# Moving one chunk's normalisation, some stores and one signal, and cutting a GpSimd addition in four, in a long-convolution and feed-forward block

## What is computed

```python
xn = (x - mean) / sqrt(var + 1e-5)
proj = xn @ in_proj_w + in_proj_b            # 256 -> 768
v = proj[..., :256]
for i in range(2):                           # two long convolutions
    v = fft_conv(v, filter_i)                # filter from a small MLP with exp(-|decay| t) window
    xc = depthwise_conv3(ctrl_i) + kb        # ctrl_i is the i-th other third of proj
    v = v * (xc * sigmoid(xc @ gate_w[i] + gate_b[i]))
attn = v @ out_proj_w + out_proj_b
tern(w), scale(w) = clip(round(w / s), -1, 1), s = mean(|w|, axis=1)
h = xn @ (tern(w_fc) * scale).T + gate * (xn @ v.T @ fast_b.T @ u.T)
ffn = relu(h)**2 @ (tern(w_proj) * scale).T
out = x + attn + ffn
```

## Time and profile before

| | us |
|---|---|
| three runs | 881.22, 882.63, 882.59 |
| median | 882.59 |
| the profiled execution | 882.74 |
| its span in the trace | 880.8 |
| TensorE busy | 837.3 (95%) |
| VectorE busy | 621.8 (71%) |
| ScalarE busy | 471.4 (54%) |
| GpSimd busy | 238.6 (27%) |

### The profile page before, as it was taken

One profiled execution on the slowest core, in us unless ns is written; L12 is line 12 of the kernel. 1 busy time (PEld: TensorE's weight loads), 2 busy tenths in 40 slices (PEclk: granted clock), 3 DMA queues, 4 the chain that ended last, 5 costly groups with the idle time before them and its releaser, 6 DMA issues.

```text
span 880.8 us, 25943 instructions
## 1 busy us (share of the span) xinstructions
PE 837.3 (95%) x9920; PEld 695.4 (79%) x9921; DVE 621.8 (71%) x1041; ACT 471.4 (54%) x698; POOL 238.6 (27%) x248
## 2 busy tenths in 40 slices
PE   8779999999999997999999999999999999999997
PEld 3468888888888866878888888777887787788997
DVE  7849988988999884565665566566546656666887
ACT  6757777787877763444435353434444444444221
POOL 4445646655664402021112112111011201200000
PEclk9989999999999999999999999999999999999999
DMA  8762243234323268768767778677887876952896
GB/s 217 235 217 97 96 149 138 95 103 162 116 95 138 102 165 242 156 138 196 173 162 156 189 167 197 124 168 181 181 151 171 180 174 115 202 111 47 221 314 209
DMA packets 90687, 142.03 MB, mean 161 GB/s; under 512 B 12861, under 2 KB 70606, under 8 KB 89742
## 3 DMA queue, kind: packets, MB, share of 16 engines
q1 hardware_dynamic: 72990, 101.80, 48.7%
q0 software_dynamic: 7728, 28.05, 10.0%
q10 hardware_dynamic: 9920, 11.54, 4.0%
HBM read 97.39 MB, written 43.97 MB: 160 GB/s over the span
## 4 chain that ended last, share of the span: by engine, by line
PE 47%; DVE 9%; issue 4%; ACT 1%; DMA 1%; DVEq 0%; POOL 0%; ACTq 0%; POOLq 0%
PE pp L1372 13%; PE py L1391 13%; PE pf L1341 11%; DVE r L1163 3%; PE pf L1347 3%; PE py L1428 2%; PE py L1359 2%; DVE pp L1153 2%; DVE r_lo L1168 1%; DVE GC L1158 1%; DVE xb L1158 1%; PE pp L457 1%; PE pp L459 1%; PE pp L458 1%; ACT r_hi L1275 1%
## 5 line engine op out<-in xcount | busy, mean ns | idle before, releaser
L1275 ACT ACTIVATE r_hi<-r 128x512 fp32r<-128x512 f32 x128 | 80.9, 632 | 149.4 <-DVE r L1163 149.4
L1391 PEld LDWEIGHTS py<-vwin,lead 64*64 64x64 f32 x5120 | 132.9, 133 | 25.2 <-issue 25.2
L1372 PE MATMUL pp<-wproj,r_hi 128*128 128x256 f32 x512 | 135.3, 297 | 14.6 <-DVE r_lo L1168 10.4
L1270 ACT ACTIVATE r<-pf,fscale 128x512 f32<-128x512 f32 x128 | 87.8, 686 | 111.5 <-PE pf L1347 111.4
L1391 PE MATMUL py<-vwin,lead 64*64 64x128 f32 (+4 forms) x5120 | 146.9, 265 | 0.5 <-issue 0.5
L1168 DVE TENSOR_TENSOR r_lo<-r,r_hi 128x512 fp32r<-128x512 f32 x128 | 93.1, 727 | 67.2 <-ACT r_hi L1275 67.1
L1341 PE MATMUL pf<-tokens,split_a 128*128 (+1 forms) x512 | 139.6, 394 | 0.9 <-issue 0.9
L1372 PE MATMUL pp<-wproj,r_lo 128*128 128x256 f32 x512 | 126.7, 281 | 0.0
L1372 PEld LDWEIGHTS pp<-wproj,r_hi 128*128 128x128 f32 x512 | 96.1, 188 | 32.1 <-DVE r_lo L1168 14.3
L498 POOL TENSOR_SCALAR lead<-lead,norms 128x256 f32<-128x256 f32 x64 | 117.8, 1851 | 3.4 <-POOL norms L492 3.4
L660 DVE SCALAR_TENSOR_TENSOR xc<-ctrl,taps,xc 128x512 f32<-128x512 f32 x128 | 96.8, 776 | 18.8 <-ACT xc L766 18.1
(11 more groups left out here) (189 smaller groups left out, 1531.1 us busy)
## 6 DMA issues: line engine op xcount, KB each, us to landing
lead<-filters SPq DMA_DIRECT2D x128, 320.0 KB, 6.2
xnT_hbm<-split_b SPq DMA_DIRECT2D x32, 512.0 KB, 3.3
tokens<-xnT_hbm POOLq DMA_DIRECT2D x30, 512.0 KB, 5.1
lead<-in_attn_x SPq DMA_DIRECT2D x16, 512.0 KB, 4.1
gc_hbm<-xc SPq DMA_DIRECT2D x16, 512.0 KB, 2.6
GC<-gc_hbm SPq DMA_DIRECT2D x32, 256.0 KB, 6.3
out<-GC ACTq DMA_DIRECT2D x15, 512.0 KB, 6.4
GC<-in_attn_x POOLq DMA_DIRECT2D x9, 512.0 KB, 7.5
```

The source lines that it names most:

```text
L1270: act.activation(r[j][:, :], pf[:, j, :], ACT.Relu, scale=fscale[:, m:m + 1]).then_inc(relu_done, 1)
L1275: act.activation(r_hi[j][:, :], r[j][:, :], ACT.Copy).then_inc(r_hi_done, 1)
L1372: last = pe.matmul(pp[:, i, :], part[m % 2][:, i * P:(i + 1) * P], wproj[:, m, :], start=(m == 0 and n == 0 and i % 2 == 0), stop=(m == HT ...
L1391: last = pe.matmul(py[g % 2][q * BW:(q + 1) * BW, side, l, :, A:NB], tile[rows, q * PAIR + l, j * BW:(j + 1) * BW], vwin[g % 2][rows, q, l ...
```

## The change

In setup, the statistics of chunk 1 are taken by VectorE and its normalisation is done by GpSimd, which gets the second set of small values (`norms0`) for chunk 0; the step before the first of the project stage loses both. ScalarE takes the sums of |w_fc| for three of eight row tiles, VectorE for five, and GpSimd the thresholds. The low part of chunk 0 is made after the ternary values of w_proj, and ScalarE copies both halves of the turned w_proj. The scales and v_t are stored from parts of GC1 that no load of the next stage writes, in a new order, and are counted with the large stores (`STORES`), which the project stage waits for later; SyncE waits only for the two stores of zeros. In mix, `y_out` is raised ahead of the memsets, the wait for `srow_in` goes into `scale`, and GpSimd's bias addition becomes four instructions of 128x256.

```diff
-STORES = 10
+STORES = 12
...
-        srow = sb("scale_row", [1, D])
+        srow = Gf[0:1, 7 * L + 7 * HID // 4:7 * L + 7 * HID // 4 + D]
...
-        vrank = sb("vstack", [P, KT, PARTS, RANK], F32R)
+        vrank = Gf[:, 7 * L + 3 * HID // 2:7 * L + 3 * HID // 2 + KT * HALF].bitcast(F32R).rearrange("p (k s r) -> p k s r", k=KT, s=PARTS)
+        norms0 = sb("norms0", [P, TT, 11])
...
+        ACT_SUMS = 3
...
-            sp.wait_ge(srow_ready, 1)
-            load(scales, srow[0:1, :], small_stored)
-            sp.wait_ge(vrank_ready, 1)
-            load(v_t, vrank[:, :, :, :].bitcast(F32), small_stored)
             sp.wait_ge(ranks_ready, 1)
             load(u_t, ranks.bitcast(F32), stored)
             by_input_row = projT.rearrange("p (m d) -> p m d", m=HT)
...
+            sp.wait_ge(proj_ready, 1)
+            load(proj_t[:, 0:HT // 2, :], by_input_row[:, 0:HT // 2, :], stored)
+            sp.wait_ge(srow_ready, 1)
+            load(scales, srow, stored)
+            sp.wait_ge(vrank_ready, 1)
+            load(v_t, vrank.bitcast(F32), stored)
+            sp.wait_ge(proj_ready, 2)
+            load(proj_t[:, HT // 2:HT, :], by_input_row[:, HT // 2:HT, :], stored)
+            sp.wait_ge(small_stored, 16 * 2)
             sp.wait_ge(proj_in, 16 * PROJ_LOADS)
...
+            pool.wait_ge(abs_summed, ACT_SUMS)
+            pool.wait_ge(fc_summed, 1)
+            pool.tensor_scalar(fsc[:, :], fsc[:, :], 1.0 / D, 1e-5, ALU.mult, ALU.max).then_inc(uscale_step, 1)
+            pool.wait_ge(uscale_step, 1)
+            pool.tensor_scalar(fth[:, 0:HT], fsc[:, :], 0.5, None, ALU.mult).then_inc(uscale_step, 1)
+            pool.tensor_scalar(fth[:, HT:2 * HT], fsc[:, :], -0.5, None, ALU.mult).then_inc(uscale_step, 1)
+            rstd0(pool, 0, True)
+            normalise0(pool, 0, 0)
...
+            rstd(pool, 1)
+            normalise(pool, 1, 1)
...
-            statistics(dve, 0, 0, True)
             dve.wait_ge(fc_in, 16)
-            link(dve.tensor_reduce(fsc[:, :], fc_nat, AX.X, ALU.add, apply_absolute_value=True))
-            scales_of(fsc, fth, HT, D)
+            dve.tensor_reduce(fsc[:, ACT_SUMS:HT], fc_nat[:, ACT_SUMS:HT, :], AX.X, ALU.add, apply_absolute_value=True).then_inc(fc_summed, 1)
+            statistics0(dve, 0, 0, True)
+            statistics(dve, 1, 1, True)
+            dve.wait_ge(uscale_step, 3)
+            below(fc_nat, fc_tern, fth, HT, slice(0, D))
             dve.reciprocal(finv[:, :], fsc[:, :]).then_inc(finv_ready, 1)
-            below(fc_nat, fc_tern, fth, HT, slice(0, D))
             dve.wait_ge(filter_in, 16 * FILTER_LOADS)
-            link(dve.tensor_scalar(ndec[:, :], dec[:, :], -1.0, None, ALU.mult))
-            link(dve.tensor_tensor(ndec[:, :], ndec[:, :], dec[:, :], ALU.min))
+            link(dve.scalar_tensor_tensor(out=ndec[:, :], in0=dec[:, :], scalar=-1.0, in1=dec[:, :], op0=ALU.mult, op1=ALU.min))
...
-            dve.wait_ge(xn_hi_done, 1)
-            dve.wait_ge(xnT_done, 1)
-            dve.tensor_tensor(xn[1][:, :, :], xnT[:, :, :], xn[0][:, :, :].bitcast(F32), ALU.subtract).then_inc(xn_split, 1)
             for h in range(2):
                 cols = slice(h * HID // 2, (h + 1) * HID // 2)
                 below(pr_nat, pr_tern, pth, KT, cols)
                 above(pr_nat, pr_tern, pth, KT, cols)
+            dve.wait_ge(xn_hi_done, 1)
+            dve.wait_ge(xnT_done, 1)
+            dve.tensor_tensor(xn[1][:, :, :], xnT[:, :, :], xn[0][:, :, :].bitcast(F32), ALU.subtract).then_inc(xn_split, 1)
...
-            dve.wait_ge(projT_mm, 2)
-            dve.wait_ge(proj_ready, 1)
-            dve.tensor_copy(projT[:, L // 2:L], lower[:, L // 2:L]).then_inc(proj_ready, 1)
...
+            act.wait_ge(fc_in, 16)
+            for m in range(ACT_SUMS):
+                act.activation(h1[:, m * D:(m + 1) * D], fc_nat[:, m, :], ACT.Abs, accum_out=fsc[:, m:m + 1]).then_inc(abs_summed, 1)
...
-            act.wait_ge(projT_mm, 1)
-            act.activation(projT[:, 0:L // 2], lower[:, 0:L // 2], ACT.Copy).then_inc(proj_ready, 1)
+            for h in range(2):
+                cols = slice(h * L // 2, (h + 1) * L // 2)
+                act.wait_ge(projT_mm, h + 1)
+                act.activation(projT[:, cols], lower[:, cols], ACT.Copy).then_inc(proj_ready, 1)
...
             pe.wait_ge(xnT_done, 1)
-            pe.wait_ge(xn_split, 1)
+            pe.wait_ge(xn_hi_done, 1)
...
-                if s0 + 2 < NCH:
+                if 0 <= s0 and s0 + 2 < NCH:
                     rstd(pool, s + 2)
                     normalise(pool, s + 2, s0 + 2)
...
                 if s0 < 0:
-                    statistics(dve, 1, 1)
...
-                pool.tensor_tensor(buf, buf, bo_row[:, :].unsqueeze(1).broadcast_to([P, TT, D]), ALU.add).then_inc(xb_biased, 1)
+                for i in range(TT):
+                    row = buf[:, i, :]
+                    last = pool.tensor_tensor(row, row, bo_row[:, :], ALU.add)
+                last.then_inc(xb_biased, 1)
...
-            for rows in (ranks, zs):
-                dve.memset(rows[HALF:P, :].bitcast(F32), 0.0).then_inc(rest_zero, 1)
+            dve.sem_inc(y_out, 2)
             dve.memset(lowmask[:, :], 0.0).then_inc(mask_zero, 1)
             dve.wait_ge(mask_zero, 1)
             dve.memset(lowmask[2 * RANK:3 * RANK, :], 1.0).then_inc(mask_ready, 1)
-            dve.sem_inc(y_out, 2)
+            for rows in (ranks, zs):
+                dve.memset(rows[HALF:P, :].bitcast(F32), 0.0).then_inc(rest_zero, 1)
...
-            dve.wait_ge(srow_in, 16)
-
             def scale(it):
+                dve.wait_ge(srow_in, 16)
                 dve.wait_ge(proj_mm, it * HT + HT + 2)
```

More of the change, by code:

```diff
@@ L49, with setup_stage @@
 HALF = PARTS * RANK
-def setup_stage(nc, hbm, ident, bv_row, flag, V, GC1, Wv, Win, Wgate, eps, half, load_x, load_taps, norm, tern, ranks, fscale, stored, xn, xnT, x0, xn_ready, first_done):
+def setup_stage(nc, hbm, ident, bv_row, flag, V, GC1, Wv, Win, Wgate, eps, half, load_x, load_taps, norm, norms, tern, ranks, fscale, stored, xn, xnT, x0, xn_ready, first_done):
     (in_w, in_b, out_b, freqs, w1, b1, w2, b2, w3, b3, decay, gate_w, fast_b, w_fc, w_proj, u, v, gate,
@@ L130, in setup_stage @@
         projT_mm, proj_ready, srow_mm, srow_ready = sem("projT_mm"), sem("proj_ready"), sem("srow_mm"), sem("srow_ready")
-        psum_ready, psc_ready, finv_ready, uscale_step = sem("psum_ready"), sem("psc_ready"), sem("finv_ready"), sem("uscale_step")
+        abs_summed, psc_ready, finv_ready, uscale_step = sem("abs_summed"), sem("psc_ready"), sem("finv_ready"), sem("uscale_step")
+        fc_summed = sem("fc_summed")
+        ACT_SUMS = 3
         x0T = ps[:, 4:4 + KT, :]
@@ L134, in setup_stage @@
         hi_ready, eps_ready, vrank_ready = sem("hi_ready"), sem("eps_ready"), sem("vrank_ready")
-        statistics, rstd, normalise = norm
+        statistics0, rstd0, normalise0 = norm(norms0)
+        statistics, rstd, normalise = norm(norms)
         ctx.enter_context(nc.allow_non_contiguous_dma(reason="a few small vectors, one value a partition"))
@@ L360, in _ @@
             for k in range(KT):
-                act.activation(junk[:, k, :], pr_nat[:, k, :], ACT.Abs, accum_out=psc[:, k:k + 1]).then_inc(psum_ready, 1)
+                act.activation(junk[:, k, :], pr_nat[:, k, :], ACT.Abs, accum_out=psc[:, k:k + 1]).then_inc(abs_summed, 1)
             act.wait_ge(xT_mm, 1)
@@ L367, in _ @@
             act.wait_ge(m1_mm, 1)
-            act.activation(vrank[:, :, :, :], ps[:, 6, 0:KT * RANK].rearrange("p (k r) -> p k r", k=KT).unsqueeze(2).broadcast_to([P, KT, PARTS, RANK]),
+            act.activation(vrank, ps[:, 6, 0:KT * RANK].rearrange("p (k r) -> p k r", k=KT).unsqueeze(2).broadcast_to([P, KT, PARTS, RANK]),
                            ACT.Identity, scale=gcol[:, :]).then_inc(vrank_hi_done, 1)
@@ L1519, in conv_ffn_kernel @@
             dve_passed, pool_passed = (weights.enter_context(nc.semaphore(n)) for n in ("dve_norm_passed", "pool_norm_passed"))
-            norm = norm_steps(xt, norms, eps, half, x_loaded, stat_done, aggr_done, rstd_step, xn_ready, dve_passed, pool_passed)
+            norm = lambda values: norm_steps(xt, values, eps, half, x_loaded, stat_done, aggr_done, rstd_step, xn_ready, dve_passed, pool_passed)
             bias_in = weights.enter_context(nc.semaphore("bias_in"))
@@ L1563, in conv_ffn_kernel @@
             peaks = weights.enter_context(nc.sbuf_tensor("peaks", [P, 2, 4], F32))
-            setup_stage(nc, hbm, ident, bv_row, flag, V, GC1, Wv, Win, Wgate, eps, half, load_x, load_taps, norm,
+            setup_stage(nc, hbm, ident, bv_row, flag, V, GC1, Wv, Win, Wgate, eps, half, load_x, load_taps, norm, norms,
                         xm[:, 0, :, :, :].rearrange("p s k t -> p (s k t)"), xm[0:HALF, 1, 0, :, :].rearrange("p k t -> p (k t)"), fscale, stored, xn, xnT, xt[0], xn_ready, first_done)
```

(2 more changed lines are left out.)

10 lines of the change are left out of this document (4 added, 6 removed).

## The result

The changed kernel takes 871.76 us, median of 870.36 to 874.30 over four runs, against 882.61 before: ratio 0.9883, 95% interval 0.9854 to 0.9913. That is 10.9 us faster; 868 was forecast, 14.5 faster. The profiled execution took 873.15 us, with a span of 871.2 against 880.8. Runs of one kernel lie further apart than I had assumed: 3.9 us over these four, and 10.8 us (875.23 to 886.00) over 23 runs of the kernel before on another chip. So for anything under 2 us I look at traces, and at several of them where I can, since each trace is one execution.

A forecast was written before the change was run, and what follows sets the result against it. The prediction took TensorE's idle time as the bound: waits for VectorE's low part in mix and the borders into project and mix. Terms 8.6 + 1.9 + 4.0 = 14.5 us off 882.74 gave 868, range 863.5 to 874.

The forecast's parts named there:

- 42.9 + 0.84: Border from setup to project: setup ends at 42.9 instead of 46.94 us, and the border itself costs 0.84.
- A square is held until GpSimd's addition ends, and the pieces let VectorE in: Mix stage: a blocked square waits for the rest of one piece only; 7 to 10 us come back, 8.6 taken.
- the example: Mix iteration at 728.81 us: square 1.87 us late, 1.41 reaching TensorE; with pieces 0.22 late, about 0.3 reaching TensorE.
- Mix start, 1.9 us: Border into mix: early `y_out` saves 1.2 to 1.7 us, and L1172's wait of 0.45 goes too.
- Setup, 4.0 us: Setup's end: rearranged work and stores end the stage at 42.9 instead of 46.94 us; bounds 2.5 to 5.8.
- Sum: Whole kernel: 8.6 + 1.9 + 4.0 = 14.5 us against the profiled 882.74, so 868.
- the mix term: Mix stage: the gain from the bias addition in four pieces, 8.6 us.
- rival 2: Border to project: GpSimd or something placed too early ends setup, giving 0.5 to 2 us, 870.5 to 872; chance 0.14.
- Rivals 1 and 3: Mix: pieces hold VectorE as one, 877 to 882, chance 0.16; the same with dear pieces, slower, up to 899, 0.05.

The follow-up runs named there:

- the timed kernel without the pieces: The changed kernel with GpSimd's bias addition in one piece again: 880.72 us over 12 runs, ratio 0.9992 (0.9972 to 1.0012).
- the two-piece run: The changed kernel with the bias addition in two instructions of 128x512 instead of four of 128x256: 872.95 us, ratio 0.9891.
- the kernel with eight: The changed kernel with the bias addition in eight instructions of 128x128 instead of four of 128x256: 869.34 us, ratio 0.9864.

## Why the start of mix gave nothing

**The signal and the moved wait alone,** in the kernel before:

```diff
-            for rows in (ranks, zs):
-                dve.memset(rows[HALF:P, :].bitcast(F32), 0.0).then_inc(rest_zero, 1)
+            dve.sem_inc(y_out, 2)
             dve.memset(lowmask[:, :], 0.0).then_inc(mask_zero, 1)
             dve.wait_ge(mask_zero, 1)
             dve.memset(lowmask[2 * RANK:3 * RANK, :], 1.0).then_inc(mask_ready, 1)
-            dve.sem_inc(y_out, 2)
+            for rows in (ranks, zs):
+                dve.memset(rows[HALF:P, :].bitcast(F32), 0.0).then_inc(rest_zero, 1)
...
-            dve.wait_ge(srow_in, 16)
-
             def scale(it):
+                dve.wait_ge(srow_in, 16)
```

> The kernel before with y_out ahead of the memsets and the wait for the scales in scale, nothing else. Theory (TensorE cannot begin the mix stage earlier, whatever the signal does): its first product comes 3.40 us after its last one, as before, and the time is within 1 us of the kernel before. Rival (the signal does set it, and something else in the full change takes it back): the first product 1.5 us earlier and 1.5 to 2 us gained.

Measured: ratio 1.0003 (0.9983 to 1.0024). The timeline:

```profile
336.01 1.51 PE L1358 MATMUL py<-tokens,split_b 128*64 128x512 f32 x3 [3.41 <-issue]
```

3.41 us again, in twelve profiled executions between 3.40 and 3.52 where no spare product stood ahead. The rival falls.

**What holds TensorE there?** First probe: three spare products of 512 columns at the start of its mix block and three behind the branch (`pe.If(tail < 1)`), in the changed kernel.

```diff
...
+            for _ in range(3):
+                pe.matmul(pf[:, 0, :], ident[:, :], Vprobe, start=True, stop=True)
             pe.sem_inc(fc_mm, HT)
...
             tail = pe.value_load(flag[0:1, 0:1], min_val=0, max_val=1)
...
             def stages(far):
+                for _ in range(3):
+                    pe.matmul(pf[:, 1, :], ident[:, :], Vprobe, start=True, stop=True)
```

> The changed kernel with three spare products at the very start of TensorE's mix block and three more behind its branch on the flag, none waiting for a semaphore. Theory (TensorE has to read the flag and take a branch, and what follows it comes late): the first three start about 1.5 us after the last product of the project stage, the other three only with rank, 3.4 us or more after it. Rival (rank waits for data, the tokens or vrank): all six come early, and only rank starts 3.4 us after.

```profile
332.21 2.81 PE L1342 MATMUL pf<-GC,ident 128*128 128x512 f32 x6 [1.43 <-PEq L524]
334.86 2.74 PE L1464 MATMUL pf<-GC,ident 128*128 128x512 f32 x6
```

The first three do start 1.43 us after the stage before, but they last so long that the next three follow without a gap, and the probe hides what it was to show. It took 876.30 us in its one run. I made the second with eight columns a product and four places.

```diff
...
+            pe.matmul(pf[:, 0, 0:8], ident[:, :], spare, start=True, stop=True)
             pe.sem_inc(fc_mm, HT)
...
             def stages(far):
+                pe.matmul(pf[:, 0, 0:8], ident[:, :], spare, start=True, stop=True)
...
                 pe.wait_ge(vrank_in, 16)
+                if first:
+                    pe.matmul(pf[:, 0, 0:8], ident[:, :], spare, start=True, stop=True)
                 pe.wait_ge(y_out, it * GPI + 2)
                 if first:
+                    pe.matmul(pf[:, 0, 0:8], ident[:, :], spare, start=True, stop=True)
                     pe.wait_ge(first_in, 32)
```

> The changed kernel with four spare products of eight columns on TensorE: at the start of its mix block, behind the branch on the flag, behind rank's wait for vrank, and behind its wait for y_out. Theory (reading the flag and branching): the first starts 1.4 us after the last product of the project stage, and the second, third and fourth together 3.3 us after it, with rank right behind. Rival (data): the second comes before 2.5 us, and one of the later gaps holds the rest; which one names the wait.

```profile
330.80 0.36 PE L1341 MATMUL pf<-GC,ident 128*128 128x8 f32 x2 [1.43 <-PEq L524]
332.70 0.59 PE L1465 MATMUL pf<-GC,ident 128*128 128x8 f32 x2 [1.54 <-issue]
333.14 0.57 PE L1369 MATMUL pf<-GC,ident 128*128 128x8 f32 x2
333.56 0.57 PE L1372 MATMUL pf<-GC,ident 128*128 128x8 f32 x2
333.99 1.95 PE L1379 MATMUL py<-tokens,split_b 128*64 128x512 f32 x4
```

Behind the border's 1.43 us, the whole delay lies between the first and the second: 332.70 - 330.80 = 1.90 us. The waits for vrank, `y_out` and the tokens cost nothing; each later product follows at the pace of the probe. 1.43 + 1.90 = 3.33, which is the 3.40 but for 0.07. What TensorE's sequencer does in the 1.90 us stands in the same trace, under the lines of the source (ns, shortest, median, longest, then the start):

```profile
L1342 PEldq EVENT_SEMAPHORE  x1: 51/51/51, 330.8 to 330.8; - x1
L1345 PEldq TENSOR_LOAD <-flag x1: 890/890/890, 331.3 to 331.3; - x1
L1345 PEldq FUSED_REGOPS  x1: 168/168/168, 332.2 to 332.2; - x1
L1482 PEldq COMPARE_BRANCH  x2: 86/1972/3858, 332.6 to 862.6; - x2
```

About 0.5 us go to the first probe and three semaphore signals (from L1342 on), 0.89 us to the load of the flag, 0.4 to working on the register, and 0.09 to the branch, the first of the two at L1482. So it is the load above all. In the kernel before the same load took 0.858 us, in the changed kernel 0.867. The Trainium skill (Runtime: NRT & Kernel Launch, "Instruction fetch mechanics") says that a taken branch to a target outside the fetched window forces a fetch. No such fetch shows here: the branch starts at 332.6 and the next product at 332.70.

## Why setup gave so little

The profile shows SyncE late with its issues. Four runs take the possible causes apart.

**Normalisation back in the project stage,** in the changed kernel:

```diff
-            rstd(pool, 1)
-            normalise(pool, 1, 1)
...
-                if 0 <= s0 and s0 + 2 < NCH:
+                if s0 + 2 < NCH:
```

> The changed kernel with GpSimd's normalisation of chunk 1 back in the step ahead of the project stage. Theory (DMA backlog): SyncE's last issues are as slow as in the changed kernel, the first product stays between 46 and 47.5, time within 1 us. Rival (GpSimd's normalisation slows SyncE's issues, or its end sets the border): issues of 0.3 to 0.7 us and a first product before 44.5.

Measured: 871.03 us, ratio 0.9890 (0.9854 to 0.9925). SyncE's queue and the first product:

```profile
38.44 1.96 SPq L146 DMA_DIRECT2D u_t<-tokens  x1
40.44 2.10 SPq L146 DMA_DIRECT2D proj_t<-GC  x1
42.59 1.86 SPq L146 DMA_DIRECT2D scales<-GC  x1
```

```profile
47.15 0.76 PE L469 MATMUL pc<-split_b,split_a 128*128 128x512 f32 x1 [8.00 <-PEq L55]
```

As slow without GpSimd at work. Moving the normalisation neither helps nor harms, within the error.

**The last four stores from ScalarE's queue,** in the changed kernel:

```diff
-            sp.wait_ge(proj_ready, 1)
-            load(proj_t[:, 0:HT // 2, :], by_input_row[:, 0:HT // 2, :], stored)
...
             act.activation(sigmoid_table[:, :], eps[:, 0:1], ACT.Sigmoid)
+            act.wait_ge(proj_ready, 2)
+            for h in range(2):
+                ms = slice(h * HT // 2, (h + 1) * HT // 2)
+                act.dma_start(proj_t[:, ms, :], by_input_row[:, ms, :]).then_inc(stored, 16)
+            act.wait_ge(srow_ready, 1)
+            act.dma_start(scales, srow).then_inc(stored, 16)
+            act.wait_ge(vrank_ready, 1)
+            act.dma_start(v_t, vrank.bitcast(F32)).then_inc(stored, 16)
```

> The changed kernel with the last four stores of setup (both halves of proj_t, the scales, v_t) issued from ScalarE's queue after its last activation. Theory (SyncE's issues are slow because the DMA engines are behind with the filters' stores, whatever queue asks): the four issues take long from ScalarE's queue too, more than 1 us each for the large ones, and the first product of the project stage comes at 45 or later. Rival (only SyncE's own queue is full): they take 0.3 to 0.7 us each, and the first product comes near 44.5.

Measured: 871.73 us, ratio 0.9901 (0.9863 to 0.9938). ScalarE's queue:

```profile
39.73 2.18 ACTq L385 DMA_DIRECT2D proj_t<-GC  x2
41.96 1.92 ACTq L387 DMA_DIRECT2D scales<-GC  x1
43.92 0.85 ACTq L389 DMA_DIRECT2D v_t<-GC  x1
```

The store of 1 KB takes 1.92 us to issue from this queue too. It is not SyncE's queue alone that is full. Of the forecast, the first product at 45 or later came (45.52). The two large ones took over 1 us on average, but not each: 0.35 and 1.80 us one by one.

I read it as a backlog of the DMA engines. Their share is 0.99 from 38 to 42 before and 0.98 after, so they are as busy in both kernels. From 24 to 46 they moved 5.63 MB before and 5.99 MB after, nearly all of it the filters, fc_t, u_t and proj_t. The change asks for the transfers earlier and without a pause, and they do not come much faster. Not every small store is slow: with the same setup stage, the 1 KB took between 0.29 and 1.78 us to issue, and the border came at 45.74 and 46.05 in the two traces with 0.29. What stays is the sum of the issues. Which part of the engines' path holds an issue is open.

**The four stores deferred.** In the variant with the normalisation back, they are issued in the project stage, behind the first two stores of xn, where `stored` is waited for only later.

```diff
-            sp.wait_ge(proj_ready, 1)
-            load(proj_t[:, 0:HT // 2, :], by_input_row[:, 0:HT // 2, :], stored)
-            sp.wait_ge(srow_ready, 1)
-            load(scales, srow, stored)
-            sp.wait_ge(vrank_ready, 1)
-            load(v_t, vrank.bitcast(F32), stored)
-            sp.wait_ge(proj_ready, 2)
-            load(proj_t[:, HT // 2:HT, :], by_input_row[:, HT // 2:HT, :], stored)
+            later.append(lambda sp: [sp.dma_start(dst, src).then_inc(stored, 16) for dst, src in (
+                (proj_t[:, 0:HT // 2, :], by_input_row[:, 0:HT // 2, :]), (proj_t[:, HT // 2:HT, :], by_input_row[:, HT // 2:HT, :]),
+                (scales, srow), (v_t, vrank.bitcast(F32)))])
...
+                if s0 < 0:
+                    load_ahead[3][0](sp)
```

> The changed kernel with the normalisation of chunk 1 back in the project stage and the last four stores of setup issued there too, behind the first two stores of xn. Theory (the border waits for SyncE to get rid of these issues): the first product comes at 42 to 43, 4 to 5 us earlier, TensorE idles about 3.5 us instead of 8 and has at most as many slow products, and 3.5 to 5.5 us are gained over the changed kernel, 866 to 868. Rival (the stores come back in the project stage, as late loads or a late wait for `stored`): less than 1 us gained.

Measured: 867.22 us (864.81 to 871.46), ratio 0.9847 (0.9814 to 0.9881), on the chip where the variant without deferring took 871.03: 3.8 us less (the intervals of the two ratios overlap; five of the six runs lie below all four of the other variant). The queue and the first product:

```profile
44.87 2.49 SPq L199 DMA_DIRECT2D proj_t<-GC  x2
```

```profile
41.92 0.47 PE L464 MATMUL pc<-split_b,split_a 128*128 128x512 f32 x1 [3.17 <-PEq L55]
```

The issues are as slow as ever, and no border waits for them. The border stands at 41.92, 5.2 us earlier than in the changed kernel's trace and 3.8 us earlier than in any other with the changed setup, and 1.8 us ahead of the 42.9 + 0.84 of the prediction. So the issues are what held the border. This kernel has the lowest median of the study.

**Six spare products at the end of setup,** in that kernel, to keep the clock up:

```diff
+            pe.wait_ge(ranks_ready, 1)
+            for _ in range(6):
+                pe.matmul(ps[:, 4, :], ones[:, :], h2[:, 0:512], start=True, stop=True)
```

> The kernel with deferred stores (defer_norm_back) and six spare products of 512 columns on TensorE at the end of setup, whose results nobody reads. Theory (the idle time ahead of the project stage is what takes the clock down there): the granted clock stays at 1.00 over the border, the nine or so products at half the clock are gone, and 1.5 to 2 us more are gained, ratio about 0.983. Rival (the clock falls there anyway, or the products delay the border): the same number of slow products, no gain.

```profile
38.65 5.32 PE L455 MATMUL ps_setup<-GC,ones 128*128 128x512 f32 x12
44.56 0.47 PE L467 MATMUL pc<-split_b,split_a 128*128 128x512 f32 x1 [0.60 <-PEq L55]
```

Measured: 869.18 us, ratio 0.9865 (0.9831 to 0.9898), no gain. The clock theory holds in this trace: the granted clock stays at 2.4 GHz over the border, and the products of the first chunk start every 0.23 us from the second on. But each spare product took 0.89 us, and the border came 2.6 us later. Its 24 products start within 5.3 us instead of 6.9, so the clock gives back 1.6 us, and TensorE then waits 0.68 us for VectorE's `peaks`, which it did not before. That doesn't pay for the 2.6: the next transposition comes at 53.47 instead of 51.55. Two or three spare products would fit into the 3.17 us of idle time; whether they would keep the clock up was not run.

## Point by point

- *A square is held until GpSimd's addition ends, and the pieces let VectorE in.* Right. Pieces of 0.747 us against my 0.74, the example's square late by 0.33 against 0.22. The second collision, with the low part, came too: 0.35 us at TensorE in the example against my 0.3. But between 440 and 765 only 4 places of 9 were left, and the waits fell by 8.4 us (10.0 to 1.6); from 330 on by 8.8 (10.4 to 1.6). The mix stage got 545.3 - 535.8 = 9.5 us shorter, inside my 7 to 10 and above the 8.6. What I left out is that GpSimd is held in turn; it cost nothing.
- *Mix start, 1.9 us.* Wrong: 0. The step that failed is the register read, which was covered by the wait before and for which I allowed at most 0.4 us (1.63 less 1.2) once the signal was early. With the signals ahead of it and the branch it takes 1.90 us, and with the border it fills the same 3.40 us that the late signal filled: two causes of one length, of which the trace named only one. The wait of 0.45 for L1172 went, and a gap of 1.0 us without a named cause came in the group's convolution, at 345.22; that gap is open.
- *Setup, 4.0 us.* The step that failed is SyncE's queue: I took its issues at the durations of the rows before, 0.25 to 0.71 us, where they were 1.21 to 2.16. Those rows came from a queue that had just paused for 2.7 us; now it asks without a pause, against the backlog shown above. The order of work on VectorE, TensorE, ScalarE and GpSimd came out as forecast or up to 1.9 us earlier (ScalarE done at 41.5 instead of 42.9, GpSimd at 42.6 inside my 40.9 to 43.7). In the profiled pair four more products also ran at half the clock, and the first transposition of chunk 1 stands at 57.89 against 57.66, so 0.2 us later; in eight other traces with this setup or one near it it stands at 55.2 to 57.7, against 58.3 and 58.4 in two with the old one. So setup gives between nothing and some 2 us, and the timed kernel without the pieces puts it at 0.7 with an error of 1.8.
- *Sum.* 14.5 forecast, 10.9 measured. In the profiled pair the mix term is 0.9 more and the other two are 5.9 less, which gives 9.5; the spans differ by 9.6, and the other 1.3 is run-to-run scatter. The time of 871.76 lies in my range of 863.5 to 874 because the pieces were right and the range was wide enough for the loss of the other two terms. My rival 2, "the border moves little", is what happened, for a cause I had only named in passing. That the time fell into its 870.5 to 872 is in part luck: it still counted 1.9 us for the start of mix, and the larger mix term and the scatter made up for them. (By its own terms, 882.74 - 8.6 - 1.9 less 0.5 to 2, and 0.15 lower for the median, it should have read 870.1 to 871.6.) Rivals 1 and 3 fall with the two-piece run.

## What to carry to other kernels

Where VectorE is on the critical path and GpSimd is not, try cutting GpSimd's two-input instructions; here two pieces gave nearly all of it, and in the kernel with eight no wait was left. GpSimd's own total grows (here from 2.39 to 3.74 us where it met VectorE), so see that its consumer comes late enough. Before moving work out of the way of a border, list for each engine what it must get done there at the load it will then have, DMA issues too, and push behind the border whatever nobody needs at once. A wait with a named releaser may hide a second one of the same length.

## What I had not expected of the hardware

- While VectorE works between two of GpSimd's additions, the next addition is held: 1.72 us instead of 1.28 for a piece of 128x512, 1.18 and 1.19 instead of 0.72 and 0.75 for one of 128x256, in the two places shown.
- A DMA issue of 1 KB took 1.25 us in the changed kernel, 1.86 with the normalisation moved back and, from ScalarE's queue, 1.92, where the kernel before took 0.25. The DMA share near 1 does not tell the two apart.
- Reading one flag from memory next to the engines (SBUF) into a register cost TensorE 0.86 to 0.89 us at the start of a block.
- The number of products at 1.2 GHz after the border does not follow the idle time: 9 after 4.62 us, 13 after 8.16, but also 13 after 2.49 and 7 after 7.29. After 0.60 us there was none.
